# Head projections in two rounded parts, one sub-step later, and four smaller edits in a transformer tower on one core

## The chip, the cores and the metric

One Trainium2 chip, one of its cores. The metric is the device time of one execution in microseconds (us), the median of several runs. The five engines are named as the profile names them: PE (matmul) with PEld (its weight loads), DVE (vector), ACT (scalar), POOL (GpSimd) and SP, whose queue (SPq) issues most of the transfers.

## The reference, cut to what matters

```python
def reference(x, cls_tok, ...):                      # x: (32, 64, 256, 4)
    h = _L0_tok_ref(x, ...)                          # token mixer -> (32, 256, 256)
    h = concat([broadcast(cls_tok), h], axis=1)      # 257 rows
    h = h + _L0_attn_ref(_layernorm(h), ...)
    return h + _L0_ffn_ref(_layernorm(h), ...)       # shared and routed experts

def _L0_tok_ref(x, Wq_w, ...):
    q, k, v = proj(Wq), proj(Wk), proj(Wv)           # 64x64 weights, four heads of 64
    ew, ek = exp(w_bias * local_mask), exp(k)
    y = sigmoid(q) * (ew @ (ek * v)) / (ew @ ek)
    h = y @ out_w + out_b + flatten(x)
    return layernorm(h) * ln_g + ln_b

def _L0_attn_ref(x, ...):                            # 16 heads of 16
    def holo_linear(x, basis, phase, amp):
        resonance = einsum('bli,hi->blh', x, basis)  # 256 -> 32
        return einsum('blh,oh->blo', resonance, amp * cos(phase))   # 32 -> 256
    q, k, v = holo_linear(x, q...), holo_linear(x, k...), holo_linear(x, v...)
    return holo_linear(softmax(q @ k.T / 4) @ v, o...)
```

The second `einsum` of `holo_linear`, for q, k and v, is what is called a head projection below.

## The kernel before, in words

The kernel has two stages. Stage A (`stage_a`, up to some 1180 us of the span) does the token mixer and the attention, one batch of 256 rows after another, 32 of them, and writes its rows to DRAM (`hscr`). Stage B does the experts. The change touches stage A alone.

Stage A is a software pipeline. Step b runs from b = -3 to 32, and each step has sixteen **sub-steps** n = 0 to 15. In sub-step n of step b PE does the scores of two heads of batch b and DVE takes the row maxima of batch b+1 (n up to 12) or b+2 (n from 13). Between them lie pieces of the mixer of batch b+3, of the projections of batch b+2 and of the output of batch b-1. On each engine the order of a step is written out by hand (`step` in each engine's block); engines meet at semaphores only, and each engine executes strictly in the order written.

What lies around the change, in the order of a step:

- `mixer_q` (L366, n = 1): eight products of a 128x128 weight with 256 columns. The split input `xh` holds the rounded x on rows 0 to 63 and its remainder on rows 64 to 127. POOL makes it (`split_x`, L1057 to 1063).
- `turn` (L415, n = 2): transposes z, which ACT wrote in `attn_norm` (L698, n = 1), into bank 6; ACT copies it to zT (L662). `turn_values` (L512, n = 1 and 2) turns the attention's values; ACT copies the class column of `og` in `keep_class` (L685, n = 0).
- `mixer_kv` (L376, L379, n = 2 and 3): a bias product and eight products of 128 columns; ACT takes the exponent into `ek` (L658), DVE multiplies (`mixer_ekv`, L782).
- `resonances` (L421, n = 3): z by the basis, 96 rows; ACT copies them into rT (L732) as f32.
- `heads_qk` (L431, n = 4 for q and n = 5 for k): two f32 products of Wz and rT with 256 columns, into bank 6. ACT rounds the result into qhi or khi (`high`, L668); DVE subtracts it to get the remainder qlo or klo (`low`, L830), and that frees bank 6 for the next projection. `heads_v` (L438, n = 11) is the third.
- `turn_back`, `out_resonances` (L525, n = 4) and `attend_out` (L531, n = 5): the output of batch b-1. ACT copies onT (L743) before L525.
- `mixer_sum` (L390, n = 4 and 5): two sums over the key rows. DVE takes the reciprocal of the first in two halves (`mixer_inverse`, L788, n = 5), and makes y from both (`mixer_y`, L795 and L798, n = 7).
- `mixer_out` (L398, L400, L403, n = 8 and 9): a bias product and four products with the identity, which need no y, and four with y.
- `maxima` (L468) and `scores` (L485) of the sub-steps; a second pair of banks for maxima, one pair for scores, so that scores of one sub-step wait for the exponent (L675) of the one before. `values` (L497, L502) at n = 0, 6, 10, 13.

**The transfers of the heads.** SP spreads q and k of batch b+2 over the rows that PE's maxima and scores use. The order of its queue in a step is: the second half of k of batch b+1; two transfers of the class row; `spread_q` of batch b+2, six transfers; the row block of batch b-1 to DRAM; the first half of k of batch b+2 (`spread_k`, six transfers); two loads of x; two of the shifts. `spread_q` begins with this wait, which counts both remainders, q and k:

```python
        def spread_q(j, p):

            sp.wait_ge(lo_ok, 2 * j + 2)
```

and the first maxima of batch b+2, on PE at n = 13 of step b, wait for both sets of transfers:

```python
            if i == 0:
                pe.wait_ge(q_in, 16 * DMAS * (m + 1))
                pe.wait_ge(k_in[0], 16 * DMAS * (m + 1))
```

DVE's order at n = 4 to 7 is: the row maxima of n = 4; the remainder of q; a remainder of the output (L825); then at n = 5 the first reciprocal, the remainder of k, the residual sum (L871), the second reciprocal; at n = 6 a row maximum; at n = 7 y.

Of the kernel before, what the change touches and what calls it, by code (L numbers as in the profile page):

```python
# [15 lines left out]
F32 = mybir.dt.float32  # L16
# [53 lines left out]
def stage_a(nc, ctx, sem, a, hscr, mv3, rs3, eye, mhalf, ps):  # L70
# [10 lines left out]
    def temp(*shape):  # L81
# [10 lines left out]
    wkv, wq, idn = temp(2, 2 * C), temp(2, 2, P), temp(C)  # L92
# [7 lines left out]
    wkvr = sb("wkvr", [P, 2, 2 * C], F32R)  # L100
    wqr = sb("wqr", [P, 2, 2, P], F32R)
# [44 lines left out]
    rT = sb("rT", [3 * HARM, NP])  # L146
# [15 lines left out]
    wo3 = temp(D)  # L162
    wos = sb("wos", [3 * HARM, D], F32R)
# [14 lines left out]
    (c_load, c_set, d_step, half_ok, mask_ok, wb_ok, ew_ok, arg_ok, cos_ok, w_ok, clsvar_ok, clsrs_ok, clsz_ok, cls_ps,  # L178
     clsT_ok, clsr_ok, spread_ok, mix_in) = (
        sem(x) for x in ("c_load", "c_set", "d_step", "half_ok", "mask_ok", "wb_ok", "ew_ok", "arg_ok", "cos_ok", "w_ok",  # L180
                         "clsvar_ok", "clsrs_ok", "clsz_ok", "cls_ps", "clsT_ok", "clsr_ok",
# [9 lines left out]
    wo_in, vb_ok, vb_in, roh_ok = sem("wo_in"), sem("vb_ok"), sem("vb_in"), sem("roh_ok")  # L191
    r_ps, r_ok, qk_ps, v_ps, v_ok, hi_ok, lo_ok = (
# [159 lines left out]
    def _(pe):  # L352
        def filler(n, count):

            for i in range(count):
                pe.matmul(ps[:, n, :], wqr[:, 0, 0, :], wqr[:].rearrange("p a b q -> p (a b q)"), start=True, stop=True)

        def mixer_q(j, p):

            pe.wait_ge(xsp_ok, j + 1)  # L360
            if not isinstance(j, int) or j >= 2:
                pe.wait_ge(cl_ok, 2 * j - 3)
            for f in range(FT):
                for hh in range(2):
                    for term in range(2):
                        last = pe.matmul(ps[:, 2, f * L:(f + 1) * L], wqr[:, term, hh, :], xh[p % 2][:, 2 * f + hh, :],  # L366
                                         start=(hh == 0 and term == 0), stop=(hh == 1 and term == 1))
            last.then_inc(q_ps, 1)

        def mixer_kv(j, p, t):  # L370

            if t == 1:
                pe.wait_ge(tq_ok, j + 1)
            elif not isinstance(j, int) or j >= 2:
                pe.wait_ge(cl_ok, 2 * j - 2)
            pe.matmul(ps[:, 3 - t, :], oner[:], browr[:, 0:H * 2 * C], start=True, stop=False, skip_group_check=True)  # L376
            for h in range(H):
                for term in range(2):
                    last = pe.matmul(ps[:, 3 - t, h * 2 * C:(h + 1) * 2 * C], xh[p % 2][:, h, t * P:(t + 1) * P],  # L379
                                     wkvr[:, term, :], start=False, stop=(h == H - 1 and term == 1),  # L380
                                     skip_group_check=True)
            last.then_inc(kv_ps, 1)
# [11 lines left out]
        def mixer_out(j, p, t):  # L394
            if t == 0:
                pe.wait_ge(y_ok, j + 1)
            o = ps[:, 3, t * D:(t + 1) * D]
            pe.matmul(o, oner[:], browr[:, H * 2 * C:], start=True, stop=False, skip_group_check=True)  # L398
            for h in range(H):
                pe.matmul(o[:, h * C:(h + 1) * C], xh[p % 2][:, h, t * P:(t + 1) * P], idr[:], start=False, stop=False,  # L400
                          skip_group_check=True)
            for f in range(FT):
                last = pe.matmul(o, rden[:, f, t * P:(t + 1) * P], outw[:, f, :], start=False, stop=(f == FT - 1),  # L403
                                 skip_group_check=True)
            if t == LT - 1:
                last.then_inc(h_ps, 1)
# [11 lines left out]
        def resonances(j):  # L418
            pe.wait_ge(zt_ok, j + 1)
            for f in range(FT):  # L420
                last = pe.matmul(ps[0:3 * HARM, 6, 0:L], basT[:, f, :], zT[:, f, 0:L], start=(f == 0), stop=(f == FT - 1))  # L421
# [12 lines left out]
        def heads_v(m):  # L434

            pe.wait_ge(lo_ok, 2 * m + 2)
            for t in range(LT):
                last = pe.matmul(ps[:, 6, t * D:(t + 1) * D], rT[:, t * P:(t + 1) * P], Wz[:, 2, :], start=True, stop=True)  # L438
            last.then_inc(v_ps, 1)
# [95 lines left out]
        def step(b, p):  # L535
            for n in range(NH):
# [69 lines left out]
        pe.wait_ge(clsz_ok, 1)  # L606
# [4 lines left out]
        for f in range(FT):  # L611
            last = pe.matmul(ps[0:3 * HARM, 5, 16:17], basT[:, f, :], zT[:, f, CLS:N], start=(f == 0), stop=(f == FT - 1))
# [3 lines left out]
        for n in range(2):  # L616
            for f in range(FT):
                pe.matmul(ps[:, 4, n * FT + f:n * FT + f + 1], Wz[:, n, f * P:(f + 1) * P], rT[:, CLS:N], start=True,
                          stop=True)
# [30 lines left out]
    def _(act):  # L650
# [60 lines left out]
        def step(b, p):  # L711
            for n in range(NH):
                if has(b):
                    exps(b, n)
                if has(b - 1):
                    if n == 0:
                        take_group(b - 1, G - 1)
                        keep_class(b - 1)
# [6 lines left out]
                if has(b + 2):  # L725
# [40 lines left out]
        act.activation(rT[:, CLS:NP], ps[0:3 * HARM, 5, 16:17].broadcast_to([3 * HARM, 2]), ACT.Copy).then_inc(clsr_ok, 1)  # L766
# [11 lines left out]
    def _(dve):  # L778
# [43 lines left out]

        def out_low(b):
# [33 lines left out]
        def normalise(b, t):  # L857
# [7 lines left out]
                              ALU.mult).then_inc(on_ok, 1)  # L865

# [20 lines left out]
        def step(b, p):  # L887
            for n in range(NH):
# [9 lines left out]
                if has(b + 2) and n == 4:  # L898
                    low(b + 2, p + 2, 0)
                if has(b - 1) and n == 4:  # L900
                    out_low(b - 1)
                if n == 5:
                    if has(b + 3):
                        mixer_inverse(b + 3, 0)
                    if has(b + 2):
                        low(b + 2, p + 2, 1)
                    if has(b - 1):
                        residual(b - 1, p - 1)
                    if has(b + 3):
                        mixer_inverse(b + 3, 1)  # L910
                if has(b + 3) and n == 7:
# [28 lines left out]
        dve.memset(Wz[:], 0.0)  # L940
        for t in negr:
# [9 lines left out]
        dve.tensor_tensor(wkvr[:, 1, :], wkv[:, 1, :], wkvr[:, 1, :], ALU.subtract)  # L951
        dve.tensor_tensor(wqr[:, 1, :, :], wq[:, 1, :, :], wqr[:, 1, :, :], ALU.subtract)
# [9 lines left out]
        dve.tensor_scalar(clsrs[:], clsmv[:, 1:2], EPS, None, ALU.add).then_inc(clsvar_ok, 1)  # L962
# [9 lines left out]
        dve.tensor_scalar(clsz[:], clsr[:], clsmv[:, 0:1], clsrs[:], ALU.subtract, ALU.mult).then_inc(clsz_ok, 1)  # L972
# [16 lines left out]
        dve.tensor_copy(Wz[2 * HARM:3 * HARM, 2, :], W[2 * HARM:3 * HARM, :]).then_inc(w_ok, 1)  # L989
        mixer_stats(0)  # L990
        dve.tensor_copy(eyer[:], eye[:])
        dve.wait_ge(clsr_ok, 1)
        dve.tensor_copy(rbc[:], rT[:, CLS:N].broadcast_to([3 * HARM, NH])).then_inc(clsr_ok, 1)
# [55 lines left out]
    def _(pool):  # L1049
        flat = lambda t: t[:].rearrange("p t d -> p (t d)")  # L1050

        def split_x(j, p):
# [7 lines left out]
            pool.wait_ge(xround_ok, j + 1)  # L1060
# [65 lines left out]
        pool.wait_ge(clsvar_ok, 1)  # L1126
# [972 lines left out]
def layout(i):  # L2099
# [6 lines left out]
    wkv, wq = z(P, 2, 2 * C), z(P, 2, 2, P)  # L2106
    both = np.concatenate([t["tok_Wk_w"].T, t["tok_Wv_w"].T], axis=1)
    for term, copies in ((0, 2), (1, 1)):
        for k in range(copies):
            wkv[k * C:(k + 1) * C, term] = both  # L2110
            for hh in range(2):
                wq[k * C:(k + 1) * C, term, hh, hh * C:(hh + 1) * C] = t["tok_Wq_w"].T
# [11 lines left out]
    o["basT"] = tiles(np.concatenate([t["attn_basis_" + n].T for n in "qkv"], axis=1))  # L2124
# [51 lines left out]
```

## Time and profile before

| | us |
|---|---|
| median of 3 runs (lowest to highest) | 2171.08 (2169.77 to 2176.59) |
| the profiled execution's own time | 2174.02 |
| its span, first to last instruction | 2172.2 |
| PE busy in the span | 2046.4 (94%) |
| DVE, ACT, POOL busy | 1388.7, 999.8, 686.8 |

Busy time of PE counts matmuls whose ends are modelled and overlap, so 94% doesn't say that the engine is at its peak. In the timeline a row is one or several merged instructions: start, length, engine, line, operation, output and inputs, count, and in brackets the idle time before the first and what ended it. Transfers are rows of SPq: the length is that of issuing them, and when they land is in the table of transfers.

### The profile page before, as it was taken

Reading aid. Unit: us, or ns where it says so; the run is one execution under the profiler, and the core shown is the slowest. Engines: PE = TensorE matmul, PEld = TensorE weight load, DVE = VectorE, ACT = ScalarE, POOL = GpSimd, SP = SyncE. Lnnn points to the kernel's source line nnn. Section 1 sums busy time; section 2 is a strip of 40 time slices with the busy share of each in tenths; the row PEclk is TensorE's granted clock in tenths of the full one; section 3 lists DMA queues with packets and bytes.
Section 4 is the critical chain, followed back from the end, with each engine's and each line's share of the span. In section 5 each row is a group of like instructions: output and inputs, shape, how many; then the busy total and the mean of one; then the engine's idle time right before and its main releaser. Section 6 shows DMA issues by size and latency. Waiting matters only on the chain. (4 is left out here: it accounts for less than half of the span.)

```text
span 2172.2 us, 42116 instructions
## 1 busy us (share of the span) xinstructions
PE 2046.4 (94%) x15430; PEld 1812.6 (83%) x15430; DVE 1388.7 (64%) x3049; ACT 999.8 (46%) x2080; POOL 686.8 (32%) x737
## 2 busy tenths in 40 slices
PE   5899999999999999999988999999999999999998
PEld 4777777778777777777766999989998888889998
DVE  7666767667677676776762655677754444445767
ACT  2155555555555545555454443322235555554332
POOL 4334243332433324333110311000013333333776
PEclk9899999999999999999999999999999999999999
DMA  2533424343343332334322444000013333333665
GB/s 72 85 58 79 81 55 84 59 84 69 67 83 60 85 72 64 83 61 82 62 50 87 159 155 151 30 21 30 30 45 105 106 105 105 106 103 118 189 183 162
DMA packets 125272, 189.22 MB, mean 87 GB/s; under 512 B 23153, under 2 KB 76418, under 8 KB 125074
## 3 DMA queue, kind: packets, MB, share of 16 engines
q1 hardware_dynamic: 101232, 134.65, 26.3%
q0 software_dynamic: 12736, 34.69, 5.6%
q10 hardware_dynamic: 11106, 17.19, 2.4%
q8 instruction: 131, 2.15, 0.4%
q14 instruction: 67, 0.55, 0.1%
HBM read 84.32 MB, written 49.58 MB: 62 GB/s over the span
## 5 line engine op out<-in xcount | busy, mean ns | idle before, releaser
L675 ACT ACTIVATE pT<-ps 128x514 f32<-128x514 f32 x512 | 304.9, 597 | 307.3 <-PE ps L485 303.7
L847 DVE TENSOR_REDUCE mx<-ps 128x2 f32<-128x512 f32 x512 | 343.3, 681 | 110.5 <-PE ps L468 110.3
L2057 POOL DMA_INDIRECT z<-zd,itab x136 | 128.8, 947 | 463.7 <-DVE itab L1968 248.2
L485 PE MATMUL ps<-q,km 114*128 114x258 f32 x1024 | 229.9, 306 | 31.8 <-ACT pT L675 31.6
L468 PE MATMUL ps<-km,q 112*128 112x256 f32 x1024 | 246.6, 328 | 13.2 <-DMA km<-klo 7.3
L485 PEld LDWEIGHTS ps<-q,km 114*128 114x128 f32 x1024 | 160.1, 190 | 82.4 <-ACT pT L675 54.0
L1307 PE MATMUL ps<-zhi,whi 128*128 128x256 f32 x1056 | 214.2, 284 | 1.4 <-issue 1.0
L468 PEld LDWEIGHTS ps<-km,q 112*128 112x128 f32 x1024 | 167.6, 192 | 54.4 <-issue 21.7
L1307 PE MATMUL ps<-zhi,wlo 128*128 128x256 f32 x1056 | 209.5, 279 | 0.0
L1307 PE MATMUL ps<-zlo,whi 128*128 128x256 f32 x1056 | 209.1, 279 | 0.0
L1335 ACT ACTIVATE sil<-ps 128x512 f32<-128x512 f32 x132 | 78.9, 598 | 234.8 <-PE ps L1307 234.8
L1100 POOL TENSOR_TENSOR rs<-rs,mhalf 128x2 f32<-128x2 f32 x32 | 22.2, 694 | 455.4 <-DVE mv L884 455.4
L1307 PEld LDWEIGHTS ps<-zhi,whi 128*128 128x128 f32 x1056 | 162.1, 190 | 2.0 <-issue 2.0
L1477 DVE TENSOR_TENSOR hlo<-ps,hhi 128x256 fp32r<-128x256 f32 x136 | 57.8, 425 | 163.5 <-ACT hhi L1455 163.5
L1307 PEld LDWEIGHTS ps<-zhi,wlo 128*128 128x128 f32 x1056 | 161.7, 189 | 0.0
L1307 PEld LDWEIGHTS ps<-zlo,whi 128*128 128x128 f32 x1056 | 161.6, 189 | 0.0
L1344 ACT ACTIVATE hhi<-uu 128x512 fp32r<-128x512 f32 x132 | 83.5, 632 | 164.0 <-DVE uu L1369 144.3
L1375 DVE TENSOR_TENSOR hlo<-uu,hhi 128x512 fp32r<-128x512 f32 x132 | 97.2, 736 | 92.2 <-ACT hhi L1344 92.2
L2076 POOL DMA_INDIRECT raws<-yd,idxs x130 | 130.3, 1002 | 80.3 <-PE ps L1307 39.0
L502 PE MATMUL ps<-pT,va 128*32 128x257 f32 x2048 | 142.0, 390 | 0.0
L1369 DVE TENSOR_TENSOR uu<-ps,sil 128x512 f32<-128x512 f32 x132 | 90.9, 689 | 75.0 <-ACT sil L1335 74.2
L788 DVE RECIPROCAL rden<-ps 128x256 f32<-128x256 f32 x64 | 112.0, 1752 | 27.2 <-PE ps L390 27.2
(322 smaller groups left out, 4878.8 us busy)
## 6 DMA issues: line engine op xcount, KB each, us to landing
yd<-raws SPq DMA_DIRECT2D x136, 128.0 KB, 1.8
q<-qhi SPq DMA_DIRECT2D x128, 129.0 KB, 4.2
km<-khi SPq DMA_DIRECT2D x256, 64.5 KB, 3.2
xs<-in_x SPq DMA_DIRECT2D x64, 256.0 KB, 4.4
z<-hscr SPq DMA_DIRECT2D x46, 256.0 KB, 2.9
raws<-in_wu SPq DMA_DIRECT2D x12, 768.0 KB, 4.8
hscr<-h SPq DMA_DIRECT2D x34, 256.0 KB, 5.1
zd<-z SPq DMA_DIRECT2D x33, 256.0 KB, 2.0
```

Source lines behind the costliest of these rows:

```text
L468: last = pe.matmul(ps[:, i % 2, k * L:(k + 1) * L], q2[p % U][0:MAXROW, QAT[g], t * P:(t + 1) * P], km[p % 2][0:MAXROW, k, g, 0:L], start= ...
L485: pe.matmul(ps[:, score_bank(b, n // 2) + k, 0:NP], km[p % 2][0:MAXROW + 2, k, g, t * P:(t + 1) * P], q2[p % U][0:MAXROW + 2, QAT[g], :], ...
L502: last = pe.matmul(ps[SLOT * j:SLOT * (j + 1), 7, 0:N], va[p % 2][:, t, h, :], pT[:, h, t, :], start=False, stop=(t == LT - 1), skip_group ...
L675: act.activation(pT[:, 2 * g:2 * g + 2, t, :], ps[:, score_bank(b, n):score_bank(b, n) + 2, 0:N], ACT.Exp, scale=HD ** -0.5).then_inc(s_ok, 1)
L788: dve.reciprocal(rden[:, f, :], ps[:, 3, f * L:(f + 1) * L]).then_inc(y_step, 1)
L847: dve.tensor_reduce(mx[:, t, 2 * QAT[g]:2 * QAT[g] + 2], ps[:, i % 2, :].rearrange("p (k l) -> p k l", k=2), AX_X, ALU.max, negate=True).t ...
L1307: last = pe.matmul(ps[:, 2 * (u % 2) + c, m * L:(m + 1) * L], w_[:, u, at:at + P], z_[:, f, :], start=(n == 0), stop=(n == len(mm) - 1))
L1344: act.activation(hhi[:, u % 2, :], uu[:, u % 2, :], ACT.Copy).then_inc(hhi_ok, 1)
L1369: dve.tensor_tensor(uu[:, u % 2, :].rearrange("p (c l) -> p c l", c=2), ps[:, 2 * (u % 2):2 * (u % 2) + 2, L:2 * L], sil[:, u % 2, :].rear ...
L1375: dve.tensor_tensor(hlo[:, u % 2, :], uu[:, u % 2, :], hhi[:, u % 2, :], ALU.subtract).then_inc(hlo_ok, 1)
L2057: pool.indirect_dma_start(zg(i), None, zd_rows, bass.IndirectOffsetOnAxis(itab[:, i:i + 1], 0)).then_inc(zg_in[i % NG], 16)
L2076: pool.indirect_dma_start(yg[q][0:rows, (t * TOP + n) * D:(t * TOP + n + 1) * D], None, yd, bass.IndirectOffsetOnAxis(idxs[0:rows, c * LT ...
```

## The change

Six edits, all in stage A:

1. **Head projections.** The resonances are no longer kept as f32. ACT rounds them into rhi (128 rows: the basis is widened by a second copy of the q part) and copies rows 32 to 63 of rhi to rows 96 to 127 of rlo; DVE subtracts to get the remainder on rows 0 to 95 of rlo (`res_low`). The weights are split once at the start into wst. A projection of q or k becomes four products of 256 columns in the rounded format in place of two in f32, v becomes six in place of two.
2. **One sub-step on.** q and k are projected at n = 5 and 6 in place of 4 and 5, and so are ACT's `high` and DVE's `low`. On DVE `res_low` stands at n = 4, the remainder of q at n = 5 between the residual sum and the second reciprocal, the remainder of k at n = 6 behind the row maximum.
3. **Paired third term.** POOL makes xp, which holds the rounded x of two heads; `mixer_q` takes six products in place of eight, `mixer_kv` four of 128 and two of 256 columns in place of eight of 128. xp has one buffer, so POOL waits for `mixer_kv` of the batch before.
4. **Class copy.** `keep_class` goes from ACT (n = 0) to DVE, behind the second `normalise` (n = 2).
5. **Output wait.** `mixer_out` waits for the reciprocals first, and for y only behind the bias and identity products.
6. **Turn.** `turn` goes behind `turn_values` at n = 2.

```diff
@@ mixer_q, mixer_kv (PE)
-                for hh in range(2):
-                    for term in range(2):
-                        last = pe.matmul(ps[:, 2, f * L:(f + 1) * L], wqr[:, term, hh, :], xh[p % 2][:, 2 * f + hh, :],
...
+                for n, x in enumerate((xh[p % 2][:, 2 * f, :], xh[p % 2][:, 2 * f + 1, :], xp[:, f, :])):
+                    last = pe.matmul(ps[:, 2, f * L:(f + 1) * L], wqr[:, n, :], x, start=(n == 0), stop=(n == 2))
...
+            for f in range(FT):
+                last = pe.matmul(ps[:, 3 - t, f * 4 * C:(f + 1) * 4 * C], xp[:, f, t * P:(t + 1) * P],
+                                 wkvr[:, 1:3, :].rearrange("p n w -> p (n w)"), start=False, stop=(f == FT - 1),
@@ mixer_out (PE)
             if t == 0:
-                pe.wait_ge(y_ok, j + 1)
+                pe.wait_ge(y_step, 3 * j + 2)
...
+            if t == 0:
+                pe.wait_ge(y_ok, j + 1)
             for f in range(FT):
@@ heads_qk, heads_v (PE)
-                pe.wait_ge(r_ok, j + 1)
+                pe.wait_ge(r_ok, 2 * j + 2)
+                pe.wait_ge(rl_ok, j + 1)
             else:
                 pe.wait_ge(lo_ok, 2 * j + 1)
+            whole, part = ((rhi, rlo), (rlo, rhi))[n]
             for f in range(FT):
-                last = pe.matmul(ps[:, 6, f * L:(f + 1) * L], Wz[:, n, f * P:(f + 1) * P], rT[:, 0:L], start=True, stop=True)
+                pe.matmul(ps[:, 6, f * L:(f + 1) * L], wst[0:3 * HARM, n, f * P:(f + 1) * P], part[0:3 * HARM, :], start=True, stop=False)
+                last = pe.matmul(ps[:, 6, f * L:(f + 1) * L], wst[:, n, f * P:(f + 1) * P], whole[:], start=False, stop=True)
...
+                mm = ((rhi, 2), (rlo, 2), (rhi, 3))
@@ step (PE)
-                    if n == 2:
-                        turn(b + 2)
...
-                    if n in (4, 5):
-                        heads_qk(b + 2, n - 4)
+                    if n in (5, 6):
+                        heads_qk(b + 2, n - 5)
...
+                if has(b + 2) and n == 2:
+                    turn(b + 2)
@@ step (ACT)
-                        keep_class(b - 1)
...
-                        act.activation(rT[:, 0:L], ps[0:3 * HARM, 6, 0:L], ACT.Copy).then_inc(r_ok, 1)
-                    if n in (4, 5):
-                        high(b + 2, p + 2, n - 4)
+                        if later(b + 2):
+                            act.wait_ge(v_ps, b + 2)
+                        act.activation(rhi[:], ps[:, 6, 0:L], ACT.Copy).then_inc(r_ok, 1)
+                        act.wait_ge(r_ok, 2 * b + 5)
+                        act.activation(rlo[3 * HARM:P, :], rhi[HARM:2 * HARM, :], ACT.Copy).then_inc(r_ok, 1)
+                    if n in (5, 6):
+                        high(b + 2, p + 2, n - 5)
@@ step (DVE)
                 if has(b + 2) and n == 4:
-                    low(b + 2, p + 2, 0)
+                    res_low(b + 2)
...
                     if has(b + 3):
                         mixer_inverse(b + 3, 0)
-                    if has(b + 2):
-                        low(b + 2, p + 2, 1)
                     if has(b - 1):
                         residual(b - 1, p - 1)
+                    if has(b + 2):
+                        low(b + 2, p + 2, 0)
                     if has(b + 3):
                         mixer_inverse(b + 3, 1)
+                if has(b + 2) and n == 6:
+                    low(b + 2, p + 2, 1)
@@ res_low, normalise (DVE)
+            dve.tensor_tensor(rlo[0:3 * HARM, :], ps[0:3 * HARM, 6, 0:L], rhi[0:3 * HARM, :], ALU.subtract).then_inc(rl_ok, 1)
...
+                dve.tensor_copy(clso[:, :, bass.ds(b, 1)], og[:, :, CLS:N]).then_inc(clso_ok, 1)
@@ start (DVE)
+        dve.memset(wst[:].bitcast(F32), 0.0)
...
+            dve.tensor_copy(wst[rows, n, :], Wz[rows, n, :])
...
+            dve.tensor_tensor(wst[3 * HARM:P, n, :], Wz[rows, n, :], wst[rows, n, :], ALU.subtract)
@@ split_x (POOL)
+            if later(j):
+                pool.wait_ge(kv_ps, 2 * j)
+            pool.tensor_copy(xp[C:P, :, :], xh[p % 2][C:P, 1:H:2, :]).then_inc(xround_ok, 1)
+            pool.tensor_copy(xp[0:C, :, :], xh[p % 2][0:C, 0:H:2, :])
```

SP's part of the program is not changed.

## Rows read from the trace of the kernel before

**Rows 1.** A stretch of stage A: busy PE, PEld, DVE, ACT, POOL; clock, DMA, GB/s.
```profile
600.00:800.00 200.00, 188.51 (x1453) 157.06 (x1452) 141.37 (x317) 109.09 (x221) 70.74 (x84) 1.00 0.35 74
```

**Rows 2.** Timeline of PE, one step (start, us, what, count, idle before).
```profile
515.98 0.40 PE L468 MATMUL ps<-km,q 112*128 112x256 f32 x2
...
522.02 0.66 PE L415 MATMUL ps<-eye,z 128*128 128x128 f32 x4 [0.57 <-ACT z L698]
...
523.18 1.00 PE L379 MATMUL ps<-wkvr,xh 128*128 128x128 f32 x8
...
527.69 1.03 PE L431 MATMUL ps<-rT,Wz 96*128 96x256 f32 x4
...
529.66 1.89 PE L390 MATMUL ps<-ewT,ek 128*128 128x256 f32 x8
...
538.83 1.11 PE L403 MATMUL ps<-outw,rden 128*128 128x256 f32 x4
...
546.16 0.48 PE L468 MATMUL ps<-km,q 112*128 112x256 f32 x2
...
549.76 0.40 PE L468 MATMUL ps<-km,q 112*128 112x256 f32 x2
```

**Rows 3.** Timeline of DVE, sub-steps 5 to 7 of the same step.
```profile
531.59 1.76 DVE L788 RECIPROCAL rden<-ps 128x256 f32<-128x256 f32 x1 [0.85 <-PE ps L390]
533.37 0.69 DVE L830 TENSOR_TENSOR klo<-ps,khi 128x512 fp32r<-128x512 f32 x1
533.98 0.68 DVE L871 TENSOR_TENSOR h<-ps,hres 128x512 f32<-128x512 f32 x1
534.58 1.75 DVE L788 RECIPROCAL rden<-ps 128x256 f32<-128x256 f32 x1
536.25 0.63 DVE L847 TENSOR_REDUCE mx<-ps 128x2 f32<-128x512 f32 x1
536.79 0.67 DVE L795 SCALAR_TENSOR_TENSOR tq<-tq,ps 128x512 f32<-128x512 f32 x1
537.49 0.69 DVE L798 SCALAR_TENSOR_TENSOR rden<-tq,rden 128x512 f32<-128x512 f32 x1
```

**Rows 4.** Timeline of SP's queue, the same step.
```profile
534.10 2.52 SPq L301 DMA_DIRECT2D q<-qhi  x4
...
541.08 1.23 SPq L313 DMA_DIRECT2D km<-klo  x2
```

**Rows 5.** Transfers issued from 534 to 545.9 us: count, KB each, median us to landing.
```profile
km<-klo SPq DMA_DIRECT2D x2, 64.5 KB, 4.5
```

**Rows 6.** Waits of PE: us in total, times, longest.
```profile
PE ps L415 <- ACT z L698: 18.2, 30, 1.6
PE ps L468 <- DMA km<-klo: 7.3, 11, 1.3
```

**Rows 7.** Timeline of ACT, sub-steps 1 and 3 of the same step.
```profile
520.89 1.08 ACT L698 ACTIVATE z<-hres,nb,rs 128x256 f32<-128x256 f32 x2
...
527.36 0.39 ACT L658 ACTIVATE ek<-ps 128x256 f32<-128x256 f32 x1 [1.36 <-PE ps L379]
527.64 0.59 ACT L743 ACTIVATE onT<-ps 128x512 f32<-128x512 f32 x1
```

**Rows 8.** Timeline of PE near the start of stage A, one long wait.
```profile
77.16 0.80 PE L468 MATMUL ps<-km,q 112*128 112x256 f32 x2 [2.78 <-DVE tick L1023]
```

**Rows 9.** PE by stretch: length, busy (instructions), granted clock, DMA share, GB/s.
```profile
74.00:76.60 2.60, 0.38 (x4) 1.00 0.05 5
76.60:83.40 6.80, 6.24 (x25) 0.50 0.01 2
...
110.70:114.10 3.40, 3.40 (x16) 0.50 0.10 29
...
445.00:449.00 4.00, 3.79 (x37) 1.00 0.02 5
```

**Rows 10.** Transfers issued from 516 to 522 us, the second half of k.
```profile
km<-klo SPq DMA_DIRECT2D x2, 64.5 KB, 2.5
```

More of the change, by code:

```diff
@@ L162, in stage_a @@
     wo3 = temp(D)
+    Wz = temp(3, D)[0:3 * HARM]
     wos = sb("wos", [3 * HARM, D], F32R)
@@ L355, in filler @@
             for i in range(count):
-                pe.matmul(ps[:, n, :], wqr[:, 0, 0, :], wqr[:].rearrange("p a b q -> p (a b q)"), start=True, stop=True)
+                pe.matmul(ps[:, n, :], wqr[:, 0, :], browr[:, 0:512], start=True, stop=True)
         def mixer_q(j, p):
@@ L377, in mixer_kv @@
             for h in range(H):
[L378 to L381, printed above, removed]
+                pe.matmul(ps[:, 3 - t, h * 2 * C:(h + 1) * 2 * C], xh[p % 2][:, h, t * P:(t + 1) * P],
+                          wkvr[:, 0, :], start=False, stop=False, skip_group_check=True)
+            for f in range(FT):
+                last = pe.matmul(ps[:, 3 - t, f * 4 * C:(f + 1) * 4 * C], xp[:, f, t * P:(t + 1) * P],
+                                 wkvr[:, 1:3, :].rearrange("p n w -> p (n w)"), start=False, stop=(f == FT - 1),
+                                 skip_group_check=True)
             last.then_inc(kv_ps, 1)
@@ L420, in resonances @@
             for f in range(FT):
-                last = pe.matmul(ps[0:3 * HARM, 6, 0:L], basT[:, f, :], zT[:, f, 0:L], start=(f == 0), stop=(f == FT - 1))
+                last = pe.matmul(ps[:, 6, 0:L], basT[:, f, :], zT[:, f, 0:L], start=(f == 0), stop=(f == FT - 1))
             last.then_inc(r_ps, 1)
@@ L437, in heads_v @@
             for t in range(LT):
-                last = pe.matmul(ps[:, 6, t * D:(t + 1) * D], rT[:, t * P:(t + 1) * P], Wz[:, 2, :], start=True, stop=True)
+                mm = ((rhi, 2), (rlo, 2), (rhi, 3))
+                for i, (x, n) in enumerate(mm):
+                    last = pe.matmul(ps[:, 6, t * D:(t + 1) * D], x[0:3 * HARM, t * P:(t + 1) * P], wst[0:3 * HARM, n, :],
+                                     start=(i == 0), stop=(i == len(mm) - 1))
             last.then_inc(v_ps, 1)
@@ L611, in _ @@
         for f in range(FT):
-            last = pe.matmul(ps[0:3 * HARM, 5, 16:17], basT[:, f, :], zT[:, f, CLS:N], start=(f == 0), stop=(f == FT - 1))
+            last = pe.matmul(ps[0:3 * HARM, 5, 16:17], basT[:, f, 0:3 * HARM], zT[:, f, CLS:N], start=(f == 0), stop=(f == FT - 1))
         last.then_inc(cls_ps, 1)
@@ L617, in _ @@
             for f in range(FT):
-                pe.matmul(ps[:, 4, n * FT + f:n * FT + f + 1], Wz[:, n, f * P:(f + 1) * P], rT[:, CLS:N], start=True,
+                pe.matmul(ps[:, 4, n * FT + f:n * FT + f + 1], Wz[:, n, f * P:(f + 1) * P], rcls[:, 0:1], start=True,
                           stop=True)
@@ L989, in _ @@
         dve.tensor_copy(Wz[2 * HARM:3 * HARM, 2, :], W[2 * HARM:3 * HARM, :]).then_inc(w_ok, 1)
+        dve.wait_ge(w_ok, 1)
+        for n in range(2):
+            rows = slice(n * HARM, (n + 1) * HARM)
+            dve.tensor_copy(wst[rows, n, :], Wz[rows, n, :])
+        rows = slice(2 * HARM, 3 * HARM)
+        chain(dve.tensor_copy(wst[rows, 2, :], W[rows, :]))
+        for n in range(2):
+            rows = slice(n * HARM, (n + 1) * HARM)
+            dve.tensor_tensor(wst[3 * HARM:P, n, :], Wz[rows, n, :], wst[rows, n, :], ALU.subtract)
+        rows = slice(2 * HARM, 3 * HARM)
+        dve.tensor_tensor(wst[rows, 3, :], W[rows, :], wst[rows, 2, :], ALU.subtract).then_inc(w_ok, 1)
         mixer_stats(0)
@@ L2105, in layout @@
     tiles = lambda m: f(m.reshape(-1, P, m.shape[1]).transpose(1, 0, 2))
-    wkv, wq = z(P, 2, 2 * C), z(P, 2, 2, P)
+    wkv, wq = z(P, 3, 2 * C), z(P, 3, P)
     both = np.concatenate([t["tok_Wk_w"].T, t["tok_Wv_w"].T], axis=1)
[L2108 to L2112, printed above, removed]
+    for k in range(2):
+        rows = slice(k * C, (k + 1) * C)
+        wkv[rows, 0] = both
+        wkv[rows, 1 + k] = both
+        for hh in range(2):
+            wq[rows, hh, hh * C:(hh + 1) * C] = t["tok_Wq_w"].T
+        wq[rows, 2, k * C:(k + 1) * C] = t["tok_Wq_w"].T
     o["wkv"], o["wq"] = wkv, wq
```

50 lines of the change are left out of this document (28 added, 22 removed).

## The prediction, made before the changed kernel was run

> **What bounds the kernel now.** I read the busy time by stretch first, then one step in the timelines of PE, DVE, ACT and SP, then PE's waits and the table of transfers. PE is busy 188.5 of 200 us in the middle of stage A, DVE 141, ACT 109 [rows 1]: by shares PE is the bound. The timeline shows what shares can't. A step lasts 515.98 to 549.76 = 33.78 us, first matmul of sub-step 0 to the same of the next step [rows 2]. Let S be the end of the first mixer sum, 529.66 + 1.89 = 531.55 [rows 2], and K the end of the remainder of k, 533.37 + 0.69 = 534.06 [rows 3]. SP issues its first transfer of q at 534.10 and the last of k at about 541.7, the second of the two that begin at 541.08 [rows 4]. Those two land after 4.5 us by their median [rows 5], so the last lands at about 546.2, and the matmul that needs it, the first maxima of sub-step 13, starts at 546.16 [rows 2]. The transfers are thus just in time: 546.16 - 534.06 = 12.1 us from K to the maxima, next to no slack. In 11 steps they were late already, 7.3 us in all [rows 6], 0.24 us for each of some 30 steps, so that a step lasts 34.02 us on average.
>
> So two loops have about the same length: PE's own work, and the ring of sub-step 0, S, K, SP's queue, landing, sub-step 13, sub-step 0. The change shortens the first and must be weighed on the second.
>
> **Sub-step 0 to S, part by part.** Before: 15.57 us.
> - Turn: PE waits at 522.02 for z, which ACT ends at 520.89 + 1.08 = 521.97 [rows 2, 7]. Behind the turn of values, PE does that turn inside the wait, and the class copy off ACT brings z about 0.11 us sooner (an estimate; its row on ACT is 0.2 us, overlapped). The mixer's k and v then start 0.47 us sooner. The two products that `mixer_q` loses lie ahead of this wait and give nothing here.
> - k and v: eight products in 1.00 us with some 0.17 us of tail [rows 2], 0.105 each. Four of these and two of 256 columns at about 0.12 make 0.65 in place of 0.84: 0.19 us, twice, 0.38.
> - The projection of q leaves sub-step 4: 1.03 - 0.17 = 0.86 us [rows 2].
> - Sum 1.71. Against it: the output resonances need onT, which ACT copies behind the second exponent of the mixer; these end 528.23 [rows 7] and move up only with k and v. PE reaches the place about 0.37 us too early and waits. Net 1.34 us; bounds 1.0 (turn gains nothing) and 1.7 (onT is not late).
> - New work on ACT (rhi, a wait for itself, the 32-row copy), two instructions of 0.4 to 0.6 us by the nearest rows (0.39 for 128x256, 0.59 for 128x512 [rows 7]): ACT is idle 1.36 us ahead of the exponent behind them [rows 7]. I take nothing; without that cover the exponent is late by what sticks out, 0 to 0.3 us. `res_low` on DVE falls into the 0.85 us idle before the first reciprocal [rows 3] and replaces the remainder of q there: nothing. The class copy on DVE, in sub-step 2 where it waits for the mixer's exponent: nothing. POOL's two copies and their wait for k and v: POOL is busy 71 of 200 us [rows 1], and the next x is a step away: nothing.
>
> **S to K.** Before 534.06 - 531.55 = 2.51 us: one reciprocal, then the remainder. After: DVE runs, without a pause, first reciprocal (1.71), residual (0.60), remainder of q (0.61), second reciprocal (1.67), row maximum (0.54), remainder of k (0.68): start to start in [rows 3], 5.81, with two hand-overs 5.9 us. PE and ACT feed it in time: the projection of k needs the remainder of q at S + 2.9, takes 0.6, ACT rounds it by S + 4.4, and DVE comes to it at S + 5.2. So the cheaper products save nothing from here on. **K comes 5.9 - 2.51 = 3.4 us later after S**, 2.05 us later in the step.
>
> **K to sub-step 13.** `spread_q` waits for both remainders, and behind it in SP's queue stand the row block and the six transfers of k. All thirteen move with K; nothing in their number or size changes. I take 12.1 us again. Bounds: 11.3 (landings somewhat quicker) and 13.4 (the longest late one, 12.1 + 1.3 [rows 6]).
>
> **Sub-step 13 to 0.** 3.60 us [rows 2], scores and exponents in turn, unchanged.
>
> The ring: 15.57 - 1.34 + 5.9 + 12.1 + 3.6 = 35.83 us against 34.02: 1.81 longer. PE's own way is shorter than that: K + 1.4 is y (y in two instructions behind K, 0.70 and 0.69 [rows 3]), then as before 546.16 - 538.83 = 7.33 to sub-step 13 [rows 2], K + 8.7. So PE would **stand still 12.1 - 8.7 = 3.4 us** in each step with no matmul at all, and all that the heads of v, the output wait and the second projection save ends there.
>
> **The clock.** Before, such gaps are rare in the steady state, and the clock is full. Where PE stood 2.78 us near the start [rows 8], the granted clock went to 0.50, 1.2 GHz, for the next 6.8 us; a shorter stretch at 0.50 lasted 3.4 us, while after the longest of the transfer waits (1.3 us [rows 6], just before 445) the clock stayed at 1.00 [rows 9]. A gap of 3.4 us is on the side of the first. At half clock 3.4 us of matmul work loses 1.7; some of the slow stretch falls into the gap or on work that waits for ACT. Bounds 0 (the clock holds) and 1.7; I take 0.9 us a step.
>
> The Trainium skill ("TensorE: Matmul & The Clock Gate", section "HAM oscillation — how this bites in real kernels") says that a loop of short bursts of matmuls with a wait for transfers between them is put back to the half clock on each pass. It speaks against this change, and [rows 8, 9] bear it out where the gap was long.
>
> **Start and end.** DVE's memset and six builds of wst, the first batches and the last step without a mixer: 3 us in all (0 to 6).
>
> **Sum.** 30 steps x (1.81 + 0.9) = 81, and 3: 84 us. The profiled execution took 2174.0, 3 above the median of the runs: 2258 on its scale, **2255 us** on that of the median.
>
> **The rivals.**
> - *The clock holds.* 30 x 1.81 + 3 = 57: 2228 us. For it: the steady state had no lost clock with waits to 1.3 us [rows 6, 9]. Against it: the gap is 2.6 times as long.
> - *The transfers land quickly, no change.* The second half of k, alone on the queues, lands after 2.5 us [rows 10]; were that so here, K to 13 would be 0.04 + 7.6 + 2.5 = 10.1, the ring 33.8, the gap 1.4 and the time about 2171. Against it: the same size of transfer takes 4.5 behind q and the row block [rows 5], and these stay in front of it. The Trainium skill ("DMA: Bandwidth & Descriptors", section "Anatomy of one DMA — SWDGE (gpsimd) path", another path than SP's) gives a transfer a fixed 2.0 us and its bytes over 436 GB/s, by estimate 2.15 us for 64.5 KB. The 2.5 us of [rows 10] are near it, the 4.5 us of [rows 5] are not, and the measurement decides.
> - *Faster.* PE's own loop decides: S comes 1.34 sooner, y follows S after 7.3 us, where it took 538.18 - 531.55 = 6.6 [rows 2, 3], but the bias and identity products, which stood between y and 538.83 [rows 2], are out of the way (0.6), so that sub-step 13 comes 1.1 to 1.4 us sooner. 30 x 1.25 = 37: 2134 us. That holds if the last transfer of k lands within 8.7 us of K, where 12.1 stand now; 7.6 of it is issuing. It would take the remainders to be done well before where I put them.
> - *The projections don't get cheaper.* It is off the ring behind S, so it changes the sum by little; only the move of q out of sub-step 4 counts.
>
> **Chances.** The clock falls 0.52, holds 0.28, no change 0.08, faster 0.12. A measurement of this kernel tells about 0.3% (6.5 us) from no change. Range: from 2190 (the clock holds, with 11.3 us for the transfers and the full 1.7 on the way to S, each in part) to 2290 (the clock loss at 1.7: 2255 + 24, and a few later landings). Left out are the two cases of no loss, 0.20.
>
> **What would show it.** Right: in a step's timeline the first row maxima of sub-step 13 wait some 3 us for the last transfer of k, PE's largest wait in stage A and about 90 us in all; the remainder of k stands behind the second reciprocal, 5.9 us after S; the queue's first transfer of q to those maxima still 12 us; granted clock below 1.00 between 200 and 1000 us; steps of 35.5 to 37 us. Wrong: if the transfers land 2.5 us after their issue, if the step is shorter than 34 us with idle PE only at exponents, or if the clock stays at 1.00 with a gap of 3 us (then 2228).

## The result, and where the time went

The changed kernel takes 2276.43 us (median of 4, 2274.48 to 2281.13) against 2172.25 us for the kernel before: ratio 1.0481, 95% interval 1.0457 to 1.0504. The forecast was 2255 us in a range of 2190 to 2290: slower, for the reason forecast, with two terms too small.

The span is 2274.8 us in place of 2172.2. Where the 102.6 us lie can be read from one instruction that stands once in every step, the issue of the transfers of q (line L301 before, L306 after; first and last start of each, 32 groups of four).

```profile
L301 SPq DMA_DIRECT2D q<-qhi x128: 546/596/1964, 58.9 to 1108.4; - x128
```

```profile
L306 SPq DMA_DIRECT2D q<-qhi x128: 546/596/2050, 65.8 to 1209.3; - x128
```

The first comes 6.9 us later. From the first to the last is 1049.5 us before and 1143.5 after, 94.0 more over 31 steps, **3.03 us a step**. What follows is 1.7 us longer. So nearly all of it lies in the steps of stage A.

One step of the changed kernel, PE's timeline, from sub-step 0 to the next (as [rows 2]; L422 is the turn, L540 the output resonances, L395 the mixer's sum, L410 the product with y, L483 the maxima, L517 the values):

```profile
525.13 0.40 PE L483 MATMUL ps<-km,q 112*128 112x256 f32 x2
...
530.92 0.66 PE L422 MATMUL ps<-eye,z 128*128 128x128 f32 x4
...
536.40 1.10 PE L540 MATMUL ps<-onT,basoT 128*96 128x256 f32 x4 [0.24 <-ACT onT L757]
537.34 1.89 PE L395 MATMUL ps<-ewT,ek 128*128 128x256 f32 x8
...
546.52 1.13 PE L410 MATMUL ps<-outw,rden 128*128 128x256 f32 x4
...
557.09 0.47 PE L483 MATMUL ps<-km,q 112*128 112x256 f32 x2 [3.09 <-DMA km<-klo]
...
557.85 1.10 PE L517 MATMUL ps<-pT,va 128*32 128x257 f32 x16
...
560.68 0.40 PE L483 MATMUL ps<-km,q 112*128 112x256 f32 x2
```

The step is 560.68 - 525.13 = 35.55 us, and the wait of 3.09 us ahead of sub-step 13 is new. S is 537.34 + 1.89 = 539.23. DVE behind it (as [rows 3]):

```profile
539.26 1.76 DVE L802 RECIPROCAL rden<-ps 128x256 f32<-128x256 f32 x1 [0.90 <-PE ps L395]
541.05 0.69 DVE L892 TENSOR_TENSOR h<-ps,hres 128x512 f32<-128x512 f32 x1
541.66 0.68 DVE L848 TENSOR_TENSOR qlo<-ps,qhi 128x512 fp32r<-128x512 f32 x1
542.26 1.75 DVE L802 RECIPROCAL rden<-ps 128x256 f32<-128x256 f32 x1
543.92 0.63 DVE L865 TENSOR_REDUCE mx<-ps 128x2 f32<-128x512 f32 x1
544.47 0.67 DVE L848 TENSOR_TENSOR klo<-ps,khi 128x512 fp32r<-128x512 f32 x1
```

K is 544.47 + 0.67 = 545.14, S + 5.91, and behind the first of these instructions none waits. SP's queue, then the landing of the last two (as [rows 4, 5]):

```profile
545.17 2.52 SPq L306 DMA_DIRECT2D q<-qhi  x4
...
552.16 1.23 SPq L318 DMA_DIRECT2D km<-klo  x2
```

```profile
km<-klo SPq DMA_DIRECT2D x2, 64.5 KB, 4.3
```

The second of the two begins at about 552.8 and lands at 557.1, where the maxima start. PE's waits in total (as [rows 6]):

```profile
PE ps L483 <- DMA km<-klo: 105.0, 32, 4.4
...
PE ps L540 <- ACT onT L757: 7.0, 29, 0.2
```

7.3 us in 11 waits have become 105.0 us in 32; the waits for z are 1.3 us in 2 in place of 18.2 in 30, those for y 3.9 us in 2 in place of 14.3 in 30.

The step shown keeps its clock. The next has it fall, as 28 of the 31 steps have: PE's timeline from sub-step 13 on, then PE by stretch in both steps and over stage A (length, busy, granted clock, DMA share, GB/s).

```profile
592.82 0.69 PE L483 MATMUL ps<-km,q 112*128 112x256 f32 x2 [3.29 <-DMA km<-klo]
...
594.09 1.96 PE L517 MATMUL ps<-pT,va 128*32 128x257 f32 x16
...
597.93 0.40 PE L483 MATMUL ps<-km,q 112*128 112x256 f32 x2
```

```profile
557.00:561.00 4.00, 3.92 (x37) 1.00 0.26 54
...
588.00:592.80 4.80, 1.52 (x11) 1.00 1.09 199
592.80:596.40 3.60, 3.58 (x23) 0.53 0.26 55
...
200.00:600.00 400.00, 348.92 (x2574) 0.95 0.37 67
600.00:1000.00 400.00, 350.06 (x2596) 0.96 0.35 66
```

Behind the wait of 3.29 us the clock stands at its lower level, 1.2 GHz, for 3.4 us: 0.53 over the 3.6 us read here. The values (L517) take 1.96 us in place of 1.10, and sub-step 13 to 0 lasts 597.93 - 592.82 = 5.11 us in place of 560.68 - 557.09 = 3.59. One fall costs 1.5 us. In the middle of stage A the granted clock is 0.95 and 0.96; it was 1.00 [rows 1].

The Trainium skill ("TensorE: Matmul & The Clock Gate", section "HAM oscillation — how this bites in real kernels") describes a loop of short bursts of matmuls that is put back to the half clock on each pass by its wait for transfers. The trace agrees in 28 of the 31 steps, with 1.5 us a fall, though PE works for some 32 us between two such waits here.

### The profile page after: what moved, and what is told of

It is laid out like the page before. It is cut to its first block and busy times, and to the rows that moved or that the text cites. A ratio compares the mean times of both kernels' runs of the same rounds, so it can differ in the third digit from the quotient of the medians.

```text
span 2274.8 us, 42089 instructions
## 1 busy us (share of the span) xinstructions
PE 2060.4 (91%) x15302; PEld 1808.3 (79%) x15302; DVE 1407.8 (62%) x3120; ACT 1007.6 (44%) x2080; POOL 725.5 (32%) x801
## 5 line engine op out<-in xcount | busy, mean ns | idle before, releaser
L483 PE MATMUL ps<-km,q 112*128 112x256 f32 x1024 | 249.0, 331 | 109.1 <-DMA km<-klo 105.0
L483 PEld LDWEIGHTS ps<-km,q 112*128 112x128 f32 x1024 | 174.6, 202 | 161.0 <-issue 133.3
L500 PE MATMUL ps<-q,km 114*128 114x258 f32 x1024 | 238.0, 315 | 31.3 <-ACT pT L690 31.2
L500 PEld LDWEIGHTS ps<-q,km 114*128 114x128 f32 x1024 | 168.5, 200 | 80.4 <-ACT pT L690 40.0
L517 PE MATMUL ps<-pT,va 128*32 128x257 f32 x2048 | 161.0, 432 | 0.0
L1445 PE MATMUL ps<-wlo,zhi 128*128 x272 | 119.9, 441 | 0.0
```

The source lines that it names most:

```text
L483: last = pe.matmul(ps[:, i % 2, k * L:(k + 1) * L], q2[p % U][0:MAXROW, QAT[g], t * P:(t + 1) * P], km[p % 2][0:MAXROW, k, g, 0:L], start= ...
L500: pe.matmul(ps[:, score_bank(b, n // 2) + k, 0:NP], km[p % 2][0:MAXROW + 2, k, g, t * P:(t + 1) * P], q2[p % U][0:MAXROW + 2, QAT[g], :], ...
L517: last = pe.matmul(ps[SLOT * j:SLOT * (j + 1), 7, 0:N], va[p % 2][:, t, h, :], pT[:, h, t, :], start=False, stop=(t == LT - 1), skip_group ...
L1445: last = pe.matmul(ps[:, i % 2, 0:2 * UH], z_[i % 2][:, 0, f * P:(f + 1) * P], w, start=(n == 0), stop=(n == len(mm) - 1))
```

## The experiments

All times are medians, and each ratio is to runs of the kernel before on the same chip. The experiments ran on three chips, on which the kernel before took 2172.44, 2174.49 and 2175.00 us, so a difference from the changed kernel's 2276.43 us can be off by some 3 us.

**Fill the gap.** The changed kernel, and PE has something to do while it waits:

```diff
                 if todo:
+                    if b >= 0 and n == MX_FIRST:
+                        filler(1, 13)
                     maxima(*todo[0])
```

> The changed kernel with 13 more matmuls of 512 columns on PE just ahead of the first maxima of sub-step 13; they write a free bank, their result is never read, and they last 13 x 0.213 = 2.8 us, less than the 3.1 us or so for which PE waits there for the last transfer of k. Theory (ring plus clock): the ring is as long as before, but the clock stays at 1.00, so that a step lasts 35.5 to 35.8 us, as the few steps without a fall do, in place of 37.2, and the time is 2222 to 2232 us. Rival (the loss is all in the ring, or elsewhere, and the clock costs next to nothing): 2270 to 2280 us, or more, as PE has more to do.

Measured: 2231.07 us, ratio 1.0271 (1.0253 to 1.0289). 45 us faster than the changed kernel by more work. PE's timeline of one such gap, PE by stretch, and the issue of q:

```profile
567.83 3.13 PE L361 MATMUL ps<-browr,wqr 128*128 128x512 f32 x13
571.29 0.48 PE L483 MATMUL ps<-km,q 112*128 112x256 f32 x2 [0.33 <-issue]
...
574.90 0.40 PE L483 MATMUL ps<-km,q 112*128 112x256 f32 x2
```

```profile
200.00:600.00 400.00, 381.86 (x2846) 1.00 0.38 69
```

```profile
L306 SPq DMA_DIRECT2D q<-qhi x128: 547/595/1743, 65.8 to 1165.6; - x128
```

The maxima still come when the transfers allow it, but sub-step 13 to 0 is 3.61 us, at clock 1.00. So the clock's share is 2276.43 - 2231.07 = 45.4 us, 1.5 us a step, and the ring with start and end the other 58.6 us. The issue of q agrees: it begins at 65.8 as in the changed kernel and takes 1099.8 us to the last in place of 1143.5.

**Transfers of q first.** The changed kernel, with another wait in SP's program:

```diff
@@ spread_q
-            sp.wait_ge(lo_ok, 2 * j + 2)
+            sp.wait_ge(lo_ok, 2 * j + 1)
@@ spread_k
+            if f == 0:
+                sp.wait_ge(lo_ok, 2 * j + 2)
```

> The changed kernel, but SP's transfers of q wait for the remainder of q alone, and those of the first half of k for the remainder of k. Nothing else moves. Theory (the queue behind the remainder of k sets the step): the thirteen transfers begin 2.65 us sooner, PE's wait ahead of sub-step 13 falls from 3.1 to 0.5 us or less, the clock stays full, a step lasts about 33.2 us, and the time is 2140 to 2160 us, below that of the kernel before. Rival (the new work on ACT, DVE and POOL makes the step long, the transfers only look late): 2255 us or more.

Measured: 2143.00 us, ratio 0.9858 (0.9840 to 0.9875). Nothing of the new work on ACT, DVE or POOL has gone, and the kernel is 133 us faster than the changed one, below the kernel before. PE's waits for the last transfer of k:

```profile
PE ps L485 <- DMA km<-klo: 15.8, 23, 1.5
```

These are 0.69 us each, where 0.5 or less was expected. The rival that blamed the new instructions is out.

**Projections back.** The changed kernel, with the projections in sub-steps 4 and 5:

```diff
@@ step (PE; on ACT high() in the same way)
-                    if n in (5, 6):
-                        heads_qk(b + 2, n - 5)
+                    if n in (4, 5):
+                        heads_qk(b + 2, n - 4)
@@ step (DVE): res_low to n == 3 ahead of mixer_ekv; low 0 at n == 4
                         mixer_inverse(b + 3, 0)
+                    if has(b + 2):
+                        low(b + 2, p + 2, 1)
                     if has(b - 1):
                         residual(b - 1, p - 1)
-                    if has(b + 2):
-                        low(b + 2, p + 2, 0)
...
-                if has(b + 2) and n == 6:
-                    low(b + 2, p + 2, 1)
```

> The changed kernel with the projections of q and k back in sub-steps 4 and 5, on PE, ACT and DVE; the remainder of the resonances is taken on DVE in sub-step 3, and the remainder of k again between the first reciprocal and the residual sum. The split format and all other edits stay. Theory: the remainder of k comes 2.4 us after the first mixer sum in place of 5.9, the ring is 32.4 us long and PE's own work 31.8, so the time is 2115 to 2135 us: all of the loss is in the place, none in the format. Rival (the split format costs more than it saves, by its waits on ACT and DVE): 2172 us or more.

Measured: 2126.35 us, ratio 0.9786 (0.9769 to 0.9803). PE's first mixer sum and DVE in one step:

```profile
604.52 1.89 PE L395 MATMUL ps<-ewT,ek 128*128 128x256 f32 x8
```

```profile
606.45 1.76 DVE L802 RECIPROCAL rden<-ps 128x256 f32<-128x256 f32 x1 [0.71 <-PE ps L395]
608.24 0.69 DVE L848 TENSOR_TENSOR klo<-ps,khi 128x512 fp32r<-128x512 f32 x1
```

S is 604.52 + 1.89 = 606.41, and K is 608.24 + 0.69 = 608.93, S + 2.5 as before the change. With the place undone, all else of the change is a gain of 46 us. PE's waits for k's last transfer are 19.4 us in 22: the ring is still a little the longer.

**The move alone.** The kernel before, with the projections in sub-steps 5 and 6 and the change's order on DVE, in f32, and no other edit.

```diff
@@ step (PE; on ACT high() in the same way)
-                    if n in (4, 5):
-                        heads_qk(b + 2, n - 4)
+                    if n in (5, 6):
+                        heads_qk(b + 2, n - 5)
@@ step (DVE), n == 5
-                    if has(b + 2):
-                        low(b + 2, p + 2, 1)
                     if has(b - 1):
                         residual(b - 1, p - 1)
+                    if has(b + 2):
+                        low(b + 2, p + 2, 0)
...
+                if has(b + 2) and n == 6:
+                    low(b + 2, p + 2, 1)
```

> The kernel before, with nothing but the move: projections of q and k in sub-steps 5 and 6 with the order of DVE that the change has, in f32, without res_low or any other edit. Theory: the first mixer sum comes 0.5 us sooner, the remainder of k 5.9 us behind it in place of 2.5, the ring is 36.7 us, the clock falls, and the time is 2270 to 2310 us. Rival (the move is harmless, the new instructions cost): 2150 to 2175 us.

Measured: 2311.02 us, ratio 1.0632 (1.0614 to 1.0650), 1 us above the range expected. PE's waits, and PE by stretch:

```profile
PE ps L468 <- DMA km<-klo: 87.2, 33, 5.5
```

```profile
200.00:600.00 400.00, 353.03 (x2515) 0.94 0.33 63
```

The move by itself costs 2311.02 - 2172.44 = 139 us; with the other edits beside it, as in the changed kernel, the time is some 35 us shorter.

**Both repairs.** Projections back and transfers of q first (both diffs above).

> Projections back in sub-steps 4 and 5 as in e3_heads_back, and the transfers of q wait for the remainder of q alone as in e2_q_first. Theory (once the ring is short, PE's own loop sets the step): PE's waits for the last transfer of k, 19.4 us in e3_heads_back, go, a step lasts 31.7 us, as those steps of e3_heads_back do that have no such wait, and the time is 2103 to 2118 us. Rival (the transfers set the step by their rate, wherever they begin): 2126 us again.

Measured: **2107.77 us**, ratio 0.9693 (0.9677 to 0.9709). PE's timeline, sub-step 0 of one step, then the maxima of sub-step 13 of the same step, which no longer wait, and sub-step 0 of the next:

```profile
580.45 0.40 PE L485 MATMUL ps<-km,q 112*128 112x256 f32 x2
...
608.60 0.47 PE L485 MATMUL ps<-km,q 112*128 112x256 f32 x2
...
612.19 0.40 PE L485 MATMUL ps<-km,q 112*128 112x256 f32 x2
```

The step is 612.19 - 580.45 = 31.74 us, PE's own loop. This version beats both kernels.

**The same with f32 projections.** Both repairs kept, the split format undone (the projections of q and k shown; v, the weights and the copies of the resonances likewise):

```diff
-                pe.matmul(ps[:, 6, f * L:(f + 1) * L], wst[0:3 * HARM, n, f * P:(f + 1) * P], part[0:3 * HARM, :], start=True, stop=False)
-                last = pe.matmul(ps[:, 6, f * L:(f + 1) * L], wst[:, n, f * P:(f + 1) * P], whole[:], start=False, stop=True)
+                last = pe.matmul(ps[:, 6, f * L:(f + 1) * L], Wzs[:, n, f * P:(f + 1) * P], rT[:], start=True, stop=True)
```

> e5_back_and_q_first with the projections in f32 as before the change: two f32 products in place of four or six, no rhi, rlo, res_low or wst. Theory: with the ring out of the way the format counts only where PE's work lies ahead of the first mixer sum, 0.39 us a step for q, with the heads of v 0.5 at most, so 10 to 16 us more than e5_back_and_q_first: 2115 to 2132 us. Rival (PE is the bound everywhere, so all that the three projections lose counts, 1.0 us a step): 30 us more, 2135 us or above. Other rival (the format gives nothing anywhere): as e5_back_and_q_first.

Measured: 2113.10 us, ratio 0.9716 (0.9700 to 0.9732), 5.3 us more than with the split format and 2 below the range. The issue of the transfers of q, as above, without and with the split format:

```profile
L305 SPq DMA_DIRECT2D q<-qhi x128: 546/596/1969, 56.5 to 1045.9; - x128
```

```profile
L306 SPq DMA_DIRECT2D q<-qhi x128: 547/596/649, 59.2 to 1038.7; - x128
```

Over 31 steps f32 takes 989.4 us and the split format 979.5, 0.32 us a step less, near the 0.39 of q alone; but the first issue comes 2.7 us later with it: splitting the weights puts DVE's statistics of the first batch at 41.10 in place of 40.00 us, and then PE waits 2.4 us once for the remainder of the resonances. The split format is worth about 5 us here, where the products it saves look like 1.0 us a step.

**The same with the old waits.** Both repairs kept, turn and the wait for y back in their old places:

```diff
@@ mixer_out
-                pe.wait_ge(y_step, 3 * j + 2)
+                pe.wait_ge(y_ok, j + 1)
@@ step (PE)
+                    if n == 2:
+                        turn(b + 2)
...
-                if has(b + 2) and n == 2:
-                    turn(b + 2)
```

> e5_back_and_q_first with turn in its old place ahead of the turn of values, and with mixer_out waiting for y ahead of its bias product, both as before the change. Theory: both waits of PE come back and count in full, 0.47 and 0.6 us a step, some 32 us more than e5_back_and_q_first: 2135 to 2150 us. Rival (what waits there is hidden behind exponents of the scores): 2103 to 2118 us.

Measured: 2142.06 us, ratio 0.9850 (0.9833 to 0.9866): 34.3 us more, as expected. PE's waits show both:

```profile
PE ps L405 <- DVE rden L812: 19.1, 32, 4.3
...
PE ps L422 <- ACT z L709: 17.2, 31, 1.0
```

Two moves of a few lines are thus worth more than six times the format.

**The changed kernel in f32.** All places as changed, only the format undone (the diff of the format as above).

> The changed kernel with its projections in f32 (no rhi, rlo, res_low or wst), in sub-steps 5 and 6 as changed, all other edits kept. Theory: behind the first mixer sum the projections are off the ring, as DVE is the one that has no pause there, so the dearer products change nothing: 2268 to 2285 us. Rival (PE's work there is on the ring): the projection of k lasts 0.4 us longer and that of q too, 12 to 25 us more, 2288 us or above.

Measured: 2269.95 us, ratio 1.0443 (1.0424 to 1.0462), 6.5 us less than with the split format. The dearer products cost nothing: they stand behind S, off the ring. Of the gain, 1.7 us lie ahead of the first issue of q (64.1 in place of 65.8) and 4.7 between the first and the last, where 7 of the 31 steps keep their clock in place of 3; why more of them keep it is not shown.

**Transfers of q first, before.** The kernel before with SP's two waits changed as above, and nothing else.

> The kernel before, with nothing but SP's waits changed: the transfers of q wait for the remainder of q alone, those of the first half of k for that of k. Theory (before, the ring and PE's own loop were about equal, the ring longer only in the 11 steps where PE waited for the last transfer of k, 7.3 us in all): the transfers begin 3.8 us sooner, those waits go and nothing else, a step lasts 33.78 us, and the time is 5 to 9 us less than that of the kernel before, 2163 to 2168 us. Rival (the ring set every step of the kernel before): 30 us less or more. Other rival (it was slack everywhere): no difference.

Measured: 2163.48 us, ratio 0.9957 (0.9943 to 0.9970), 11.5 us below the 2175.00 of the runs beside it, some more than expected; the interval is 6.5 to 12.4 us. From the first issue of q to the last it is 1042.6 us in place of 1049.5, 6.9 less, which are the 7.3 us of waits. Before the change the ring was longer than PE's loop in a few steps only.

**K ahead of the second reciprocal.** The changed kernel with one edit on DVE:

```diff
                         low(b + 2, p + 2, 0)
-                    if has(b + 3):
-                        mixer_inverse(b + 3, 1)
                 if has(b + 2) and n == 6:
                     low(b + 2, p + 2, 1)
+                if has(b + 3) and n == 6:
+                    mixer_inverse(b + 3, 1)
```

> The changed kernel with one edit on DVE: the second reciprocal goes behind the remainder of k, in sub-step 6. Theory: the remainder of k then ends 5.1 us after the first mixer sum in place of 5.9 (it now waits for PE's projection and ACT's rounding of k, no longer for DVE), y comes 0.8 us later but is not on the ring, the clock falls as before, and a step is 0.8 us shorter: 2245 to 2260 us. Rival (y and what follows it set the step): 2276 us or more.

Measured: 2217.93 us, ratio 1.0197 (1.0180 to 1.0215), 58.5 us less than the changed kernel where 16 to 31 were expected. DVE in one step, PE behind it, and PE by stretch:

```profile
549.50 1.76 DVE L802 RECIPROCAL rden<-ps 128x256 f32<-128x256 f32 x1 [0.90 <-PE ps L395]
...
554.05 0.69 DVE L848 TENSOR_TENSOR klo<-ps,khi 128x512 fp32r<-128x512 f32 x1 [0.87 <-ACT khi L683]
554.66 1.75 DVE L802 RECIPROCAL rden<-ps 128x256 f32<-128x256 f32 x1
```

```profile
557.73 1.13 PE L410 MATMUL ps<-outw,rden 128*128 128x256 f32 x4 [0.52 <-DVE rden L812]
...
566.86 0.48 PE L483 MATMUL ps<-km,q 112*128 112x256 f32 x2 [1.65 <-DMA km<-klo]
```

```profile
200.00:600.00 400.00, 362.48 (x2729) 0.98 0.39 71
```

S is 549.47, the first sum's end (DVE begins 0.03 us behind it), and K is 554.74, S + 5.27 where 5.1 was expected: the ring is as reckoned. What was wrong was "the clock falls as before". The issue of q tells by how much:

```profile
L306 SPq DMA_DIRECT2D q<-qhi x128: 547/596/1868, 65.9 to 1151.4; - x128
```

That is 1085.5 us, 14.3 less than with the gap filled (1099.8), where the shorter ring alone gives (5.91 - 5.27) x 31 = 20. By this estimate the clock costs some 6 us here, in place of 1143.5 - 1099.8 = 43.7. The trace shows two reasons. As y comes later, PE's work between y and sub-step 13 does too, so the wait there is 1.65 us in the step shown, not 3.1, and the clock holds behind it. And where the clock falls, it mostly falls earlier: between 140 and 1100 us it falls 14 times (24 times in the changed kernel), and 12 of these falls begin 2.7 to 3.9 us behind the first issue of q, about where PE's waits for the second reciprocal and for y end. One such step, PE's timeline and PE by stretch:

```profile
488.10 2.05 PE L410 MATMUL ps<-outw,rden 128*128 128x256 f32 x4 [0.52 <-DVE rden L812]
...
497.06 0.47 PE L483 MATMUL ps<-km,q 112*128 112x256 f32 x2
```

```profile
488.20:491.60 3.40, 3.40 (x13) 0.50 1.07 122
```

The slow stretch lies ahead of sub-step 13. Its maxima come at 497.06 with no wait, 11.9 us behind the first issue of q at 485.14, as long as the transfers take anyway: the slow work has used up what would have been the wait, and the step is no longer for it (34.94 us from issue to issue of q, where one without a fall, from 380.1, has 34.93). The edit makes K sooner and y later at once, and no run separates the two.

## Why the prediction was right, and where it was off

- **Two loops of equal length.** Right. With the transfers of q begun sooner the kernel before gains 11.5 us, the changed one 133.
- **Sub-step 0 to S.** Predicted 15.57 - 1.34 = 14.23 us, measured 539.23 - 525.13 = 14.10. PE waits 0.24 us for onT, and no longer for z ahead of the turn.
- **New work on ACT.** Taken as hidden; it was. ACT's timeline in the same step:

```profile
533.88 0.39 ACT L744 ACTIVATE rhi<-ps 128x256 fp32r<-128x256 f32 x1 [0.27 <-PE ps L428]
534.30 0.42 ACT L746 ACTIVATE rlo<-rhi 32x256 fp32r<-32x256 f32 x1
535.47 0.39 ACT L673 ACTIVATE ek<-ps 128x256 f32<-128x256 f32 x1 [0.76 <-PE ps L384]
```

  ACT is still idle 0.76 us behind the two, ahead of the exponent that mattered.
- **S to K.** Predicted 5.9 us, measured 5.91, without a pause on DVE, as listed. Two small errors cancelled: the first reciprocal is 1.78 us from start to start in [rows 3], not 1.71, so the list adds up to 5.88, and the two hand-overs, taken as 0.09, are one of 0.03.
- **K to sub-step 13.** Predicted 12.1 us, measured 557.09 - 545.14 = 11.95. The rival with quick landings (2.5 us) is out: they took 4.3. Over the middle steps of this trace the whole, from the first issue to the last landing, takes 11.3 to 12.7 us, 11.9 at the median, within the bounds of 11.3 and 13.4. The Trainium skill's 2.0 us and bytes over 436 GB/s ("DMA: Bandwidth & Descriptors", section "Anatomy of one DMA — SWDGE (gpsimd) path", another path than SP's) give 2.15 us by estimate; the measurement decides.
- **The ring.** Predicted 35.83 us, measured 35.55 in the step shown. With the gap filled, which leaves the ring alone, first to last issue of q is 1099.8 us against 1049.5 before: 1.62 us a step, where 1.81 was predicted.
- **The gap.** Predicted 3.4 us with no matmul, measured 105.0 / 32 = 3.3.
- **The clock: the term that was mis-sized.** I took 0.9 us a step, "some of the slow stretch falls into the gap or on work that waits for ACT", between 0 and 1.7. It measured 45.4 / 30 = 1.5, by filling the gap, and 1.52 in the step shown. The slow stretch began when PE resumed, and hardly any of it was hidden: 1.52 of the 1.7 us that 3.4 us of work lose at half the clock. That is 0.6 x 30 = 18 of the 21 us that the forecast missed; start and end add 5.6, and the ring takes 4 back. That part of a slow stretch can be hidden was right in itself: the last experiment shows it, where the clock falls ahead of the wait and not behind it.
- **Start and end.** Taken as 3 us, 6.9 and 1.7 by the trace, above the bound of 6. With the projections back, the first issue of q comes at 63.5 us in place of 65.8, so 2.3 of the 6.9 us lie in the later place; the other 4.6 (63.5 against 58.9 before) come with the other edits. Of these the format has 1.7 to 2.7 by the two runs without it, and splitting the weights 1.1 of that.
- **The format matters little.** Right: undoing the format in the changed kernel moved it by 0.3%, to the faster side.
- **Faster.** The edits do give the gain that this rival had, 1.1 to 1.4 us a step and more: with the place undone a step is 31.74 to some 33 us. The place of the projections took it away, together with the one wait for both remainders: undoing either brings it back.
- **What the time alone says.** The range from 2190 to 2290 us held the forecast and the rival with a clock that holds (2228). That the clock fell is told by the trace and by the filled gap, not by the time lying inside the range.

## What to carry to other kernels

Before a producer is moved to where its engine has less to do, look at what its output releases: here the longest chain ran over a queue of thirteen transfers, 12 us from the first issue to the last landing, and a later remainder of k lengthened it, while PE's 94% hid it. If one wait releases several transfers, let each wait for its own input: one wait moved and one added were worth 133 us in this place. Here a gap of PE cost its length and then the clock behind it, so a forecast that puts 3 us of idle TensorE into a loop should price both, and ask whether the slow stretch lies ahead of a wait that can take it up or behind it.

## What the runs showed that I had not expected

- Thirteen useless matmuls of 512 columns a step made the kernel 45 us faster, by keeping the clock at 1.00.
- Taking K ahead of the second reciprocal, which delays y, gained 58.5 us, some 38 more than the shorter ring accounts for (0.64 x 31 = 20). The granted clock is 0.98 over 400 us in place of 0.95, and most of the slow stretches left stand ahead of the wait for the transfers, where they cost little.
- The split format, which gave the change its name, is worth 0.32 us a step where PE is the bound and nothing where it is not; the order of two waits is worth 34 us.
